# A three-layer decoder: the opening of cross attention laid into the end of the state-space scan, and its running sums as two products

## The reference

```python
zxbcdt = h @ in_proj_w.T
z, x, Bm, Cm, dt = split(zxbcdt)
dt = softplus(dt + dt_bias);  A = -exp(A_log)
# per token: state = state * exp(dt * A) + dt * x * B;  y = state . C
yf = (y + D * x) * silu(z)
yf = yf * rsqrt(mean(yf * yf) + EPS) * norm_w
x = layernorm(x + (yf @ out_proj_w.T + mlp(h) + x))
```

```python
q, k, v = x @ wq, x @ wk, x @ wv;  k_ctx, v_ctx = ctx @ wk_ctx, ctx @ wv_ctx
out = softmax(rope(rms(q)) @ [k_ctx, k].T * scale + causal) @ [v_ctx, v]
x = layernorm(x + out @ wo)
```

## Time and profile before

| | |
|---|---|
| median of 3 runs | 824.4 us (822.17 to 825.23) |
| profiled execution | 817.42 us, span 815.7 us |
| instructions | 15022 |
| TensorE busy | 721.4 us (88%) |
| VectorE busy | 572.6 us (70%) |
| ScalarE busy | 457.5 us (56%) |
| GpSimd busy | 354.6 us (43%) |
| mean granted TensorE clock | 0.965 of full speed |

### The profile page before, as it was taken

The page is one execution under the profiler, slowest core; times in us unless marked ns, Lnnn a source line. Parts: engine busy times, 40 slices in busy tenths (PEclk is TensorE's granted clock), DMA queues, the critical chain, the costliest instruction groups (busy, mean ns, idle before and its releaser), DMA issues. The chain is left out here.

```text
span 815.7 us, 15022 instructions
## 1 busy us (share of the span) xinstructions
PE 721.4 (88%) x4930; PEld 643.4 (79%) x4930; DVE 572.6 (70%) x1173; ACT 457.5 (56%) x1002; POOL 354.6 (43%) x513
## 2 busy tenths in 40 slices
PE   4998999556899999999999998688899999999966
PEld 3887676355788888888888887567899999999855
DVE  4864777634778787878787887575477777777436
ACT  4452333235777777777777676233467777777301
POOL 0002666446997777777777774026000000000241
PEclk9999999887999999999999999889999999999978
DMA  9004200060110000000000000326556667662121
GB/s 282 1 1 146 95 1 0 0 226 1 52 34 7 0 6 3 3 6 0 6 0 0 0 1 1 100 66 236 160 170 207 222 223 241 224 210 73 39 78 52
DMA packets 45938, 64.80 MB, mean 79 GB/s; under 512 B 4288, under 2 KB 34880, under 8 KB 45632
## 3 DMA queue, kind: packets, MB, share of 16 engines
q1 hardware_dynamic: 39936, 56.39, 20.8%
q10 hardware_dynamic: 4416, 3.58, 1.6%
q0 software_dynamic: 1536, 4.20, 1.6%
HBM read 53.14 MB, written 11.01 MB: 79 GB/s over the span
## 5 line engine op out<-in xcount | busy, mean ns | idle before, releaser
L1747 POOL DMA_INDIRECT gu_raw<-rows_out,slot x16 | 15.6, 973 | 204.7 <-DMA rows_out<-y_sb 200.1
L1878 ACT ACTIVATE sg<-bg 128x256 f32<-128x256 f32 (+1 forms) x95 | 40.8, 430 | 102.8 <-PE bg L63 94.4
L1203 ACT ACTIVATE prob<-b_s,nb,rs 128x256 f32<-128x256 f32 x128 | 70.9, 561 | 37.5 <-DVE nb L1287 37.1
L61 PE MATMUL bg<-xb_hi,gu_hi 128*128 128x256 f32 x300 | 86.2, 287 | 2.7 <-DVE xb_lo L1991 2.7
L1968 DVE TENSOR_TENSOR hf<-sg,bg 128x256 f32<-128x256 f32 (+1 forms) x95 | 45.0, 474 | 60.0 <-ACT sg L1878 53.8
L1388 POOL TENSOR_SCALAR prob<-prob,rec 128x256 f32<-128x256 f32 x128 | 82.9, 665 | 6.3 <-DVE rec L1333 6.3
L63 PE MATMUL bg<-xb_hi,gu_lo 128*128 128x256 f32 x300 | 84.8, 283 | 0.0
L62 PE MATMUL bg<-xb_lo,gu_hi 128*128 128x256 f32 x300 | 84.8, 283 | 0.0
L61 PE MATMUL bd<-dn_hi,eh_hi 128*128 128x256 f32 x220 | 63.2, 287 | 3.6 <-issue 3.6
L62 PE MATMUL bd<-dn_lo,eh_hi 128*128 128x256 f32 x220 | 63.1, 287 | 3.0 <-issue 3.0
L63 PE MATMUL bd<-dn_hi,eh_lo 128*128 128x256 f32 x220 | 63.5, 288 | 2.4 <-issue 2.4
(11 more groups left out here) (300 smaller groups left out, 2609.5 us busy)
## 6 DMA issues: line engine op xcount, KB each, us to landing
gu_raw<-in_gu SPq DMA_DIRECT2D x17, 1280.0 KB
dn_raw<-in_dn SPq DMA_DIRECT2D x17, 640.0 KB
rows_in<-zero SPq DMA_DIRECT2D x1, 3840.0 KB, 14.0
rows_out<-y_sb SPq DMA_DIRECT2D x30, 128.0 KB, 2.1
x_blk<-rows_in ACTq DMA_DIRECT2D x13, 256.0 KB, 2.7
wq_raw<-in_wq SPq DMA_DIRECT2D x1, 2048.0 KB, 7.8
wkv_raw<-in_wkv SPq DMA_DIRECT2D x1, 2048.0 KB, 12.4
wo_raw<-in_wo SPq DMA_DIRECT2D x4, 512.0 KB, 3.9
```

The lines of the kernel that those rows point to most:

```text
L61: pe.matmul(out, lh, rh, start=first, stop=False)
L1203: act.activation(prob[:, g % 2, h, :], b_s[:, h // 2, (h % 2) * MW:(h % 2 + 1) * MW], ACT.Exp, bias=nb[:, h:h + 1], scale=rs[:, g, h:h + 1 ...
L1878: act.activation(sg[:, u % 3, 0:width(u)], gate_of(u), ACT.Silu).then_inc(f_sg, 1)
```

## The change

It has three parts.

1. **The sums in two products.** `dta` is split in `dta_hi` and `dta_lo` (three small VectorE instructions in block 1), GpSimd makes `tri_hi` and `tri_lo` instead of `tri`, and `sums` issues four float32r products (two halves, hi and lo) instead of two float32 calls.
2. **Orders in the scan.** TensorE's `sums` of the next even chunk moves from ahead of y of the odd chunk to behind `project_cbx`; ScalarE's `decays` for it moves behind `copies`; GpSimd does `norm_scale` and `split_chunk` of the odd step ahead of `mask_decays` and the triangles.
3. **The opening of attention in the last pair.** The class `Attention` holds the tiles and semaphores that both blocks use, laid over tiles that are dead by then (`Region`; `under_h` lies over h and the scan's weights, `under_raw` over the raw weights; PSUM tiles `two`). The turn of x stands in TensorE's queue in the step of chunk 6, three projections and the first turn of q and k in and behind the step of chunk 7; the other engines' parts are placed among the scan's last instructions. Block 3 starts with its loop, and SyncE's transfers of block 3 start there too.

```diff
@@ block 1
-                    pool.tensor_tensor(tri[:, :, :], upper..., dta[:, 0, :]...)
+                    for t, of, ready in ((tri_hi, dta_hi, 2), (tri_lo, dta_lo, 3)):
+                        pool.wait_ge(dta_ready, ready)
+                        pool.tensor_tensor(t[:, :, :], upper..., of[:, 0, :]...)
@@ scan, GpSimd
                     def triangle(n):
                         pool.wait_ge(m_seg, n)
-                        pool.tensor_tensor(tri..., upper..., dta...).then_inc(m_tri, 1)
+                        for t, of in ((tri_hi, dta_hi), (tri_lo, dta_lo)):
+                            pool.tensor_tensor(t..., upper..., of...).then_inc(m_tri, 1)
...
                     def step(j, c, first, last):
                         n = j * 2 + c
-                        if last and c:
+                        if c and last:
+                            split_chunk(j, c)
+                            norm_scale(n - 1, turn_mv)
+                        elif c:
+                            norm_scale(n - 1, turn_mv)
                             split_chunk(j, c)
                         if not (last and c):
                             mask_decays(n + 1, turn_dec)
                         if not last:
                             triangle(n + 2)
-                        if not (first and c == 0):
+                        if not (first or c):
                             norm_scale(n - 1, turn_mv)
-                        if not (last and c):
+                        if not c:
                             split_chunk(j, c)
+                        if last and c:
+                            pool.wait_ge(w_lo, BATCH)
+                            pool.memset(aw.mh[:, :], -0.5).then_inc(aw.a_const, 1)
...
+                            aw.pool_kv(pool, 0, 0)
                         pool.wait_ge(m_ve, n + 1)
...
                     over_pairs(pool, step)
-                    pool.tensor_scalar(aw.x_cur[:, :], x_tok[:, 0, :], ...)
+                    aw.pool_q(pool, 0, 0)
+                    aw.pool_roots(pool, 0, 0)
                     norm_scale(BATCH - 1, None)
+                    aw.pool_v(pool, 0, 0)
+                    aw.pool_kv(pool, 1, 1)
+                    aw.pool_roots(pool, 1, 1)
+                    aw.pool_v(pool, 1, 1)
+                    aw.pool_q(pool, 1, 1)
@@ scan, ScalarE
-                        if not (last and c):
+                        if not c:
                             decays(n + 1)
...
                         act.activation(hi, raw, ACT.Copy).then_inc(w_hi, 1)
+                        if last and c:
+                            aw.act_x(act, 0, 0)
+                            aw.act_copies(act, 0, 0)
...
                         if c and not last:
                             copies(j + 1)
+                            decays(n + 1)
                             gates(j + 1)
...
                     over_pairs(act, step)
+                    aw.act_copies(act, 1, 1)
+                    aw.act_k(act, 0, 0)
+                    aw.act_copies(act, 2, 2)
+                    act.wait_ge(w_tab, 7)
+                    aw.act_qk(act, 0, 0)
+                    aw.act_k(act, 1, 1)
@@ scan, VectorE
+                        if last and c:
+                            aw.dve_x(dve, 0)
                         dve.wait_ge(m_y, n + 1)
...
                         dve.tensor_tensor(yg[:, :, :], yd[:, :, :], sz[:, :, tk], ALU.mult).then_inc(m_yg, 1)
+                        if last and c:
+                            aw.dve_rotate(dve, 0, 0)
+                            aw.dve_squares(dve, 0, 0)
                         if not (first and c == 0):
                             norm_stats(n - 1)
...
                     over_pairs(dve, step)
+                    aw.dve_v(dve, 0, 0)
+                    aw.dve_rotate(dve, 1, 1)
+                    aw.dve_squares(dve, 1, 1)
                     norm_stats(BATCH - 1)
+                    aw.dve_v(dve, 1, 1)
                     norm(BATCH - 1)
+                    aw.dve_qk(dve, 0, 0)
@@ scan, TensorE
                         for q in range(2):
-                            mm = pe.matmul(bz[:, q, :], lower[:, :], tri[...], start=True, stop=True)
+                            for t in (tri_hi, tri_lo):
+                                mm = pe.matmul(bz[:, q, :], lower_r[:, :], t[...], start=t is tri_hi, stop=t is tri_lo)
...
                     def step(j, c, first, last):
-                        if c and not last:
-                            sums(n + 1, j * 2 + 2)
...
                         elif not last:
                             project_cbx(j + 1)
+                            sums(n + 1, j * 2 + 2)
+                        else:
+                            pe.wait_ge(w_lo, BATCH)
+                            aw.pe_project(pe, 0, 0, 0)
...
                         mm.then_inc(m_out, 1)
                         if c and not last:
                             b_dot_c(j + 1, 0)
+                        if last and not c:
+                            pe.wait_ge(m_x1, 1)
+                            pe.wait_ge(w_small, 16 * 9)
+                            pe.wait_ge(m_dec, BATCH)
+                            aw.pe_x(pe, 0, None, x_tok[:, 0, :])
+                        if last and c:
+                            aw.pe_project(pe, 0, 1, 1)
...
                     over_pairs(pe, step)
+                    aw.pe_project(pe, 0, 2, 2)
+                    aw.pe_turn_qk(pe, 0)
```

More of the change, by code:

```diff
@@ L39 @@
 MT = 2
+NS = BATCH * KVH
+QW = AREP * AD
+MW = MT * P
 RMS_EPS = 1e-6
@@ new lines, in place @@
+        self.q_r, self.k_r = r.take(AREP, AD), r.take(2, AD)
+        self.wo_raw, self.pre = r.take(AREP, DM), r.take(DM)
+        self.ss, self.sse, self.mh = r.take(AREP + 2), r.take(AREP + 2), r.take(AREP + 2)
+        self.rs = r.take(KVH, AREP + 2)
+        self.st, self.mv, self.ve, self.r1 = r.take(6), r.take(2), r.take(1), r.take(1)
+        two = [self.ps(f"two{i}", [P, 2, 512]) for i in range(4)]
+        self.bz, self.bc, self.bb, self.b_out = two[0], two[1], two[2][:, 0, :], two[2][:, 1, :]
@@ new lines, in pe_x @@
+    def pe_x(self, pe, b, n, x):
+        if not (isinstance(b, int) and b == 0):
+            pe.wait_ge(self.a_xcur, b)
+            pe.wait_ge(self.a_ctx, b * 16)
+        if n is not None:
+            pe.wait_ge(self.a_plo, n - 1)
+        for s, t in ((0, x), (1, self.c_cur)):
+            for k in range(KT):
+                mm = pe.transpose(self.x_bank(b)[:, (2 * s + k) * P:(2 * s + k + 1) * P], t[:, k * P:(k + 1) * P],
+                                  self.eye[:, :])
+        mm.then_inc(self.a_xt, 1)
```

688 lines of the change are left out of this document (329 added, 359 removed).

## The result

The changed kernel takes 826.85 us (median of 19 runs, 822.74 to 831.47), the kernel before beside it 822.61 us (19 runs, 817.23 to 827.44). The ratio is 1.0052, with a 95% interval of 1.0031 to 1.0072: some 4.3 us slower. The forecast of 825.7 was made of +1.3 us on a starting point of 824.4, which these runs put 1.8 lower; so the time was near, 1.2 us off, while the shift of 4.2 us was three times as large as its sum said. That the time came so near is luck in part: the starting point was too high by 1.8 and the shift too small by 2.9.

What follows compares the result with a forecast made beforehand. It took TensorE's nearly full queue to bound the scan, with a second chain through VectorE and GpSimd ruling its gap. Terms −0.9 +4.2 +1.0 −4.5 +1.5 = +1.3 on 824.4 gave 825.7 us, range 817 to 833.

Steps and rivals of the forecast that it cites:

- Start of the scan: First set of sums, ahead of the first projections: four cheaper products start the scan 0.9 us earlier.
- First step: First pair of chunks in the scan: no x_tok in its even half, so 21.4 us as before.
- Second and third step: Later pairs in the scan: VectorE's x_tok waits for GpSimd's split and second triangle, 23.5 us a pair, +2.1 each.
- The choice of the upper bound: Scan pairs: x_tok taken to wait out GpSimd's instructions, +4.2 for two pairs; the lower bound was +0.15 each.
- Clock in the scan: TensorE's idle gaps in the scan pairs bring half clock: +1.0 us in all, bounds 0 and 3×1.8.
- its own sign of being wrong: Scan: prediction wrong if the clock column shows tenths below 9 between 90 and 150.
- Opening: From the last pair's odd sums to attention's loop: −8.1 at full clock, −4.5 with half clock; bounds −8.1 and −3.
- Second context row: Start of attention's loop: batch 1's load queued behind the zeros makes its turn late, +1.5 us; bounds 0 and 4.
- the one by the clock: Rival, 19%: TensorE drops to half clock in each scan pair and behind the late context row; +9.6, 834.0 us.
- The faster one: Rival, 28%: port doesn't bite, clock stays up, context row in time, two of three needed; −8.7, 815.7 us.
- the −8.1 that the prediction had worked out for a full clock: Opening of attention: loop starts 35.0 instead of 43.1 us behind the last pair's odd sums, if TensorE keeps full clock.
- The one that doubted the price of the new products: Rival, 5%: a set of sums stays at 1.98 us despite the type change; +4.5 on top, 830.2 us.

Runs made afterwards that it cites:

- e4: Kernel before with the opening of attention in the last pair alone, old sums and scan orders; ratio 0.9983 (0.9960 to 1.0007).
- e8: e4 with the context row issued ahead of the zeros and VectorE's rotation and squares behind chunk 6's mean and variance; 811.18 us, ratio 0.9897.
- e12: Changed kernel plus 16 unused products on TensorE ahead of y of each odd chunk but the last; ratio 1.0049.
- e2: Changed kernel with VectorE making x_tok a step later in the scan, behind yg; ratio 1.0027.
- e11: Changed kernel with the edits of e1 (context row first), e2 (x_tok later) and e8 (seam's VectorE order); 818.19 us, ratio 0.9950.
- e13: Changed kernel with the second triangle made by ScalarE, so that GpSimd makes one; ratio 1.0066.
- e7: Kernel before with the sums as two products, old orders, the second triangle made for chunk 0 alone and reused; ratio 0.9994.
- e6: Kernel before with the sums as two products, old orders, the second triangle made by ScalarE; ratio 0.9987.
- e1: Changed kernel with SyncE issuing the context row of batch 1 ahead of the zeros into rows_in; ratio 1.0001.

## Why the prediction was near, and where its sum was off

The sum was right in most of its parts and wrong in size in three. In the order of the terms, the second number measured in the traces to "end":

- **Start of the scan, −0.9: −1.45.** Four products 0.23 apart, as worked out. The set itself starts 0.66 earlier (67.49 against 68.15), which the sum didn't have and which may be chance: e4 and e8, whose code up to there is the same, start it at 68.11 and 67.69.
- **First step, 0: +0.3**, the clock's part taken out (22.93, less the 1.43 that e12 takes back, against 21.22). The prediction saw no lock in this step; x_tok did wait there too, 0.90 instead of 0.41, until 0.14 behind the second triangle (100.03 in the changed kernel).
- **Second and third step, +2.1 each: +2.2 each at full clock.** 23.66 and 23.69 (changed, e12) against 21.45 without the lock (last steps of e2, e11, e13), itself the pair of before. The choice of the upper bound, by the row of 1.79 us in the earlier trace rows, was right; a request 0.23 us behind the split's start waited 2.31. The Trainium skill's rule (SBUF — State Buffer, section "SBUF: two separate sides") on the shared port pair, held by the one that starts first, agrees with all three of these rows.
- **Clock in the scan, +1.0: +2.2**, 1.4 in the first step (e12) and 0.8 in the third (24.45 less 23.66); none in the second. The gaps are those of the prediction (idle from 5.2 to 7.3 ahead of y of the odd chunk, 2.12 measured, and 1.8 ahead of S, 1.49 measured). What it had wrong is the number of spells: it priced a little over half a spell in three steps, and there were two. By its own sign of being wrong, a tenth below 9 in the clock column between 90 and 150, this term fails: the slice from 124 on is an 8.
- **Opening, −4.5: −3.7.** Every wait that was named is there: 2.05 for the last split, 3.47 for pre(6), the output product at half clock (3.58), ss behind projection 1. The loop starts 39.4 behind S(7), 38 to 39 were said.
- **Second context row, +1.5: +4.4, of which 0.6 comes back by "end"** (less than that stretch scatters). This is the term that was furthest off in size. I put the row at 14.4 behind the start (it was wanted at 11.2) and took 1.7 off as slack. It came at 15.6, there was no slack, and the four idle microseconds brought half clock behind them (granted 0.50 from 204 to 208). The upper bound that I gave, 4, was nearly the value.

Sum: −1.45 +0.3 +4.5 +2.2 −3.7 +4.4 −0.6 = +5.65, the shift of "end" (524.36 less 518.69). Behind it the stages are unchanged, as said.

Of the rivals, the one by the clock had the right places: its price was too high in the scan (5.4, where 2.2 was measured) and right at the context row (+2.5 beyond my term, where 2.9 was measured). The faster one needed two of its three conditions and got none, but it pointed at what was to be had: with the seam's order mended, the opening starts the loop 8.4 sooner behind S(7) (43.1 to 34.7 in e8). That this is about the −8.1 that the prediction had worked out for a full clock is chance: e8 has another order, and projection 0 runs at half clock in it (granted 0.50 from 156 to 160). The one that doubted the price of the new products is refuted by products 0.23 us apart and by e7.

## What to carry to other kernels

When a large rebuild of an opening moves the time little, look for the transfer that moved with it: a small load behind a large store on one queue comes when the store is done, and swapping two issues gave back 4.2 us. Before work is moved out of a gap of the busiest engine, ask what fills the gap then: 2 us of idleness cost 1.4 us more in the clock behind it in most pairs, and an engine with slack (here ScalarE) is a better home for added work than one that shares a port with the chain. Read the gains at several points of the timeline, since what is gained at one can be lost to the clock ahead of the next (1.8, 0.9, 0.5 and 0.2 us in e12), and here the last stage, the same code in every kernel, scattered by 7 us. And two parts that cost only together, as x_tok's place and the second triangle did, are found by taking back each.

## What the hardware showed that I had not expected

- Gaps of about 2 us on TensorE were followed by half clock in most pairs but not in all: e13 lost 1.4 us behind the gaps of 2.08 and 1.93 in two pairs (granted 0.57) and nothing behind 1.93 in the third (granted 1.00); e2 is alike (0.59, 0.58, 1.00). The changed kernel lost 1.4 behind its 2.12 and nothing behind its 1.93 ahead of y of chunk 3. Shorter gaps were hit as well: 1.49 ahead of the sums of chunk 5 in the changed kernel, 0.86 in e6.
- With the new sums, in the one execution traced of each, TensorE was at half clock in much of 68 to 72 us in six of the kernels and at 1.00 in the changed kernel, e1, e11 and e12, whose code up to that point is the same as that of e2. That put S(1) at 81.35 in e2 and at 79.27 to 79.49 in those four, 1.9 to 2.1 us apart, more than the 1.45 that the change gained there. Whether the spell belongs to a kernel or to an execution no run shows.
- The issue of a 128 KB load behind the fill of 3840 KB occupies SyncE's queue for 8.84 us; ahead of it, 0.50 us.
